# Far products of the first eight chain steps: from VectorE to GpSimd, and one order of VectorE's operations for all steps

## The chip, the cores and the metric

The kernel runs on one core of one Trainium2 chip. The core has five engines with a queue of instructions each: TensorE (PE in the profile), VectorE (DVE), ScalarE (ACT), GpSimd (POOL) and SyncE (SP, which only starts transfers here). They meet at semaphores that the program sets and waits for. The metric is the device time of one execution in microseconds. The kernel before took 275.19 us, the median of three runs (274.38 to 275.27).

## The reference, cut to what matters

The program computes two layers over 2048 tokens of width 128. Almost all of it is left alone by the change. What matters is the first layer's attention, a memory that is updated token by token:

```python
def step(M, kv):
    k_t, v_t = kv
    v_pred = jnp.einsum('bf,bfd->bd', k_t, M)
    surprise = jnp.linalg.norm(v_t - v_pred, axis=-1, keepdims=True)
    delta = k_t[:, :, None] * v_t[:, None, :]
    M = M + eta_c[None, :, None] * surprise[:, :, None] * delta
    return (_ln2(M), None)
```

`_ln2` subtracts the mean of the whole 64 x 128 matrix and divides by its deviation. Since each update is a number (the surprise) times a known outer product, the kernel never holds M in this part. It follows the surprises. They depend on inner products of keys and of values, which are known beforehand, and on the surprises of earlier tokens.

## The kernel before, in words

**Blocks side by side.** The tokens are cut into windows of L = 32 steps, which start 16 tokens apart (HALF = 16); each of the 128 partitions follows one window from a fresh start. That the windows agree where they overlap is tested afterwards (`agree`), with a general token-by-token path behind it that isn't taken. So the recurrence of 2048 tokens is a chain of 32 steps, `for j in range(L)`, with one window in each partition.

**A step of the chain.** In step j VectorE does one `tensor_tensor_scan` (L1627), which takes 18 rows of the state ST from position j to j+1 with the surprise `SG[:, j]` as factor. ScalarE waits for the scan (`scan_ready`), takes a root (L1124), and waits for VectorE's `alpha` (L1636), one number per partition; a further root gives the next surprise (L1129, `g_ready`). VectorE's remaining operations in a step spread the new surprise to later positions: `near_pairs` (L1595) adds surprise x OJN to the table Y for pairs in the same half of the window, `squares` (L1603) multiplies two rows of Y, `rows` (L1608) adds surprise x Cr to rows of ST, `mean_terms` (L1613) forms three small products. Nearly all of them read two tensors in SBUF.

**Far pairs.** Pairs with one position in the first half and one in the second are summed on TensorE. For j < FAR = 13, VectorE forms the *far product* of step j (L1690): VC[:, j] spread over 16 columns, times aT[:, j, 16:32] spread over 31 - j rows, times the surprise, (31 - j) x 16 elements, into one of three buffers FPf. TensorE adds it to PSUM bank 4 with an identity matmul (L639, `far_done`). VectorE reads the sum in step 13 (L1670, L1672), where it waits for all 13 (`far_done`, FAR).

**What sets the order.** The orders are written out by hand, one queue per engine.

- VectorE, steps j < 13: near_pairs(j), scan(j), squares(j), alpha(j), rows(0, 4), far product, mean_terms. The near pairs of a step stand ahead of its scan. From step 14 on it is another order: scan, alpha, near_pairs, rows(1, 4), squares, mean_terms, rows(0, 1), with the scan after it waiting for that last one. From step 22 on near_pairs stands ahead of alpha again, and parts of the queries (L1576) are added.
- TensorE, in step j < 13: wait for the far product, add it, then a hidden product of the expert (j < 4), then the shift matmuls `behind(k)` of `BEHIND_AT`, which carry tables of one half to the other (L607 to L617), then for j = 9 a piece of the expert's output.
- ScalarE, in step j: the roots, then `hidden` (j < 8) and copies of the shifted tables from PSUM (`BEHIND_COPY`, from j = 8).
- GpSimd does nothing between its memsets and small preparations, which end at 24.3 us, and the second layer's weights at 97.1 us.

Before the chain VectorE forms the products OJN (L1547) and OJF (L1562). Behind it stand the check of the windows, the memory's output (TensorE, L669) and the second layer from about 91 us on, where TensorE is the busiest engine.

Of the kernel before, what the change touches and what calls it, by code (L numbers as in the profile page):

```python
# [6 lines left out]
ALU = mybir.AluOpType  # L7
# [10 lines left out]
HALF = 16  # L18
S = T // HALF
L = 2 * HALF  # L20
W = S
# [26 lines left out]
FAR_BANK = 4  # L48
N_FP = 3
SB_AT = 3  # L50
LATENT = 22
# [31 lines left out]
def program(nc, a, out):  # L83
    with ExitStack() as ctx:
# [35 lines left out]
        def take(n):  # L120
            at[0] += n
            return arena[:, at[0] - n:at[0]]
# [68 lines left out]

        FPf = [take((L - 1) * HALF) for _ in range(N_FP)]
        OJF = [take((L - 1 - j) * HALF).rearrange("p (l t) -> p l t", t=HALF) for j in range(FAR, HALF)]
        b2rest = take(2 * D)[0:1].rearrange("p (i d) -> p i d", i=2)
# [53 lines left out]
        def weights_with(t):  # L248
# [35 lines left out]
        scan_ready, h_ready, alpha_ready, g_ready = (sem(n) for n in ("scan_ready", "h_ready", "alpha_ready", "g_ready"))  # L284
        fp_ready, far_done, behind_done, behind_act = (sem(n) for n in ("fp_ready", "far_done", "behind_done", "behind_act"))
        gcol_done, rh_ready, rhb_done, uw_ready, mw_done, mw_act = (
# [10 lines left out]
        tab_in, small_in, h_in = sem("tab_in"), sem("small_in"), [sem(f"h_in{i}") for i in range(2)]  # L297
        var2_ready, sd2_ready, shift_ready, xn2_act, xn2_dve, xt2_done, xt2_act = (
            sem(n) for n in ("var2_ready", "sd2_ready", "shift_ready", "xn2_act", "xn2_dve", "xt2_done", "xt2_act"))
        wvo_done, wvo_act, turn_done, skip_done, skip_act, rope_dve, turned_dve, turned_pool = (  # L300
# [67 lines left out]

        BEHIND_AT = {6: (0,), 7: (1,), 8: (2,), 10: (3,)}
        BEHIND_COPY = {8: (0,), 9: (1,), 10: (2,), 12: (3,), 13: (4,), 14: (5,)}  # L370
# [88 lines left out]
        def _(pe):  # L459
# [175 lines left out]
            for j in range(FAR):  # L635
                if j in (0, 4):
                    pe.wait_ge(eh_act, max(j, 1))
                pe.wait_ge(fp_ready, j + 1)
                mm(PS[:, FAR_BANK, j * HALF:(L - 1) * HALF], ident, FPf[j % N_FP][:, 0:(L - 1 - j) * HALF], start=(j == 0), stop=(j == FAR - 1)).then_inc(far_done, 1)  # L639
                if j < 4:  # L640
                    expert_hidden(1, j)
                for k in BEHIND_AT.get(j, ()):
                    behind(k)
                if j in EO_EARLY:
                    pe.wait_ge(eh_act, 5)
                    expert_output(0, *EO_EARLY[j])
# [303 lines left out]
        def _(act):  # L950
# [218 lines left out]
            def deviations(c):  # L1169
                piece = slice(4 * c, 4 * c + 4)  # L1170
                act.wait_ge(var2_ready, c + 1)
                f(lnt[:, 1, piece], mv[:, piece, 1], ACT.Sqrt, bias=eps2).then_inc(sd2_ready, 1)

# [150 lines left out]
        def _(pool):  # L1324
# [30 lines left out]
            nc.gpsimd.tensor_copy(b2parts[64:65, :], b2rest[:, 1, :]).then_inc(b2_ready, 1)  # L1355
            pool.wait_ge(b2_ready, 2)

            def low_part(low, value, high, rest, cols):
# [59 lines left out]
        def _(dve):  # L1418
# [160 lines left out]
            for j in range(L):  # L1579
# [36 lines left out]
                if j == HALF:  # L1616
                    dve.wait_ge(behind_act, 9)
                if j < FAR:
                    need(added)
                    dve.wait_ge(g_ready, j + 1)  # L1620
                    added = near_pairs()
                    need(formed)
                else:
                    need(max(formed, added))
                    dve.wait_ge(g_ready, j + 1)
                c = PAD + j + 1 - 2 * R_P
# [3 lines left out]

                if j < FAR and end - j - 2 > 0:
                    formed = squares()
                def alpha():
# [4 lines left out]
                if j < FAR:  # L1638
                    alpha()
                elif j == FAR:  # L1640
                    added = near_pairs()
                    alpha()
                    linear = rows(1, 4)
                elif j < LATENT:
                    if j == HALF - 1:
                        dve.wait_ge(behind_act, 6)
                    alpha()
                    if j < HALF:
                        later = Y[:, j:L - 1, HALF:L]
                        added = did(v.scalar_tensor_tensor(out=later, in0=OJF[j - FAR], scalar=sg, in1=later, op0=ALU.mult, op1=ALU.add))  # L1650
                    else:
                        added = near_pairs()
                    linear = rows(1, 4)
                    formed = squares()
                    mean_terms(linear)
                else:
                    if nb > 0:
                        added = near_pairs()
                    alpha()
                    linear = rows(1, 4)  # L1660
                    if n > 0:
                        formed = squares()
                    mean_terms(linear)

                if j == FAR:
# [6 lines left out]
                    gy = did(v.tensor_tensor(GY, GA, far_sums[:, 0:FAR, :], ALU.mult))  # L1672
                if j > FAR:
                    need(formed)
                    formed = rows(0, 1)
                    if j >= LATENT:
                        query_sums(j - LATENT)
                    continue
                if j == FAR:
                    formed = squares()  # L1680
                    need(gy)
                    formed = did(v.tensor_reduce(ST[:, R_Q, PAD + HALF - 1:PAD + L - 1], GY.rearrange("p l t -> p t l"), AX.X, ALU.add))
# [97 lines left out]
            def variances(c):  # L1780
                need(o.n)
                for n in range(4 * c, 4 * c + 4):
                    i = v.bn_aggr(mv[:, n, :], st[:, n, :])
                    (i.then_inc(var2_ready, 1) if n == 4 * c + 3 else did(i))

            def shifts(c):
                piece = slice(4 * c, 4 * c + 4)
                dve.wait_ge(sd2_ready, c + 1)
                need(did(v.reciprocal(lnt[:, 1, piece], lnt[:, 1, piece])))
                v.scalar_tensor_tensor(out=lnt[:, 6, piece], in0=mv[:, piece, 0], scalar=-1.0, in1=lnt[:, 1, piece], op0=ALU.mult, op1=ALU.mult).then_inc(shift_ready, 1)  # L1790
# [192 lines left out]
```

## Time and profile before

| | us |
|---|---|
| median of three runs | 275.19 |
| span of the profiled execution | 273.0 |
| TensorE busy in it | 258.6 (95%) |
| VectorE busy | 215.7 (79%) |
| ScalarE busy | 192.7 (71%) |
| GpSimd busy | 100.9 (37%) |

The page has no time of the profiled execution other than its span; the rest of a run's time lies outside the first and last instruction. Busy shares are means over stages with different limits. The chain that ended last goes through TensorE for 58% of the span, VectorE 30%, ScalarE 3%, GpSimd 1%; the part of it from 44.7 to 86.6 us is the chain of 32 steps. The granted TensorE clock is 0.993 of full speed on the mean. In a timeline the first number is the start of an instruction and the second how long it took. Instructions of one engine can overlap by some hundredths, so what one costs the next is read from start to start.

### The profile page before, as it was taken

Reading aid. Unit: us, or ns where it says so; the run is one execution under the profiler, and the core shown is the slowest. Engines: PE = TensorE matmul, PEld = TensorE weight load, DVE = VectorE, ACT = ScalarE, POOL = GpSimd, SP = SyncE. Lnnn points to the kernel's source line nnn. Section 1 sums busy time; section 2 is a strip of 40 time slices with the busy share of each in tenths; the row PEclk is TensorE's granted clock in tenths of the full one; section 3 lists DMA queues with packets and bytes.
Section 4 is the critical chain, followed back from the end, with each engine's and each line's share of the span. In section 5 each row is a group of like instructions: output and inputs, shape, how many; then the busy total and the mean of one; then the engine's idle time right before and its main releaser. Section 6 shows DMA issues by size and latency. Waiting matters only on the chain.

```text
span 273.0 us, 5442 instructions
## 1 busy us (share of the span) xinstructions
PE 258.6 (95%) x1792; PEld 169.9 (62%) x1796; DVE 215.7 (79%) x733; ACT 192.7 (71%) x469; POOL 100.9 (37%) x130
## 2 busy tenths in 40 slices
PE   7899999999977889999999999999999999999993
PEld 2379945466663644967877776778786444444482
DVE  6977579999999589899899988777950798666684
ACT  1497479886656479788776789998861898777730
POOL 9314000000000067898875589599775000000000
PEclk9999999999999799999999999999999999999999
DMA  7700000000000190400000000000000000000005
GB/s 199 214 15 2 2 0 4 0 1 0 2 2 0 25 413 29 154 2 4 0 2 0 2 0 1 4 0 0 2 0 2 0 1 0 4 0 0 0 18 141
DMA packets 8303, 8.51 MB, mean 31 GB/s; under 512 B 1745, under 2 KB 7378, under 8 KB 7762
## 3 DMA queue, kind: packets, MB, share of 16 engines
q1 hardware_dynamic: 7442, 7.65, 8.7%
q10 hardware_dynamic: 832, 0.49, 0.6%
q8 instruction: 16, 0.26, 0.4%
q14 instruction: 13, 0.11, 0.1%
HBM read 7.09 MB, written 1.05 MB: 30 GB/s over the span
## 4 chain that ended last, share of the span: by engine, by line
PE 58%; DVE 30%; issue 4%; ACT 3%; DMA 2%; POOL 1%; SPq 0%; DVEq 0%; ACTq 0%; POOLq 0%
PE PS L867 10%; PE PS L866 10%; PE PS L839 7%; PE PS L816 7%; PE PS L829 4%; DVE arena L1608 3%; PE PS L501 3%; PE PS L520 3%; DVE arena L1840 2%; DVE arena L1839 2%; DVE arena L1595 2%; DVE mxb L1854 2%; DVE arena L1627 2%; DVE arena L1636 2%; DMA x<-L_attn_x 2%
## 5 line engine op out<-in xcount | busy, mean ns | idle before, releaser
L866 PE MATMUL PS<-arena 128*128 128x512 f16 x128 | 48.5, 379 | 0.0
L867 PE MATMUL PS<-arena 128*128 128x512 f16 x128 | 48.5, 379 | 0.0
L1912 DVE TENSOR_TENSOR arena<-arena 128x512 f32<-128x512 f32 x32 | 22.1, 692 | 13.0 <-ACT arena L1304 13.0
L816 PE MATMUL PS<-arena 128*128 128x512 f32 (+3 forms) x80 | 31.9, 530 | 0.3 <-ACT arena L1273 0.3
L1303 ACT ACTIVATE arena<-PS,arena 128x512 f32<-128x512 f32 x32 | 22.9, 716 | 9.1 <-PE PS L867 9.1
L1368 POOL CAST arena<-arena 128x512 f16<-128x512 f32 x2 | 1.3, 644 | 72.8 <-ACT x L1166 72.8
L1360 POOL TENSOR_TENSOR arena<-arena 128x256 f32<-128x256 f32 x32 | 21.6, 674 | 15.8 <-DVE arena L1846 13.0
L1273 ACT ACTIVATE arena<-PS,lnt 128x512 f32<-128x512 f32 (+3 forms) x40 | 24.8, 628 | 3.2 <-DVE lnt L1861 3.1
L1361 POOL TENSOR_TENSOR arena<-arena,small 128x256 f16<-128x256 f32 (+1 forms) x36 | 23.8, 661 | 2.8
L1304 ACT ACTIVATE arena<-PS,arena 128x512 f16<-128x512 f32 x32 | 22.8, 714 | 0.0
L1854 DVE TENSOR_REDUCE mxb<-PS 128x1 f32<-128x512 f32 (+3 forms) x40 | 22.1, 600 | 0.0
L866 PEld LDWEIGHTS PS<-arena 128*128 128x128 f16 x128 | 12.5, 98 | 14.7
L867 PEld LDWEIGHTS PS<-arena 128*128 128x128 f16 x128 | 12.5, 98 | 14.7
L816 PEld LDWEIGHTS PS<-arena 128*128 128x128 f32 x80 | 14.0, 191 | 12.0 <-issue 9.8
L829 PE MATMUL PS<-con,arena 128*128 128x128 f32 x136 | 19.5, 273 | 0.0
L839 PE MATMUL PS<-arena,xn 128*128 128x128 f32 x144 | 19.3, 278 | 0.0
L839 PEld LDWEIGHTS PS<-arena,xn 128*128 128x128 f32 x144 | 17.7, 191 | 1.1 <-ACT xn L1257 0.2
L839 PE MATMUL PS<-arena 128*128 128x128 f32 x128 | 17.3, 278 | 0.6 <-ACT arena L1257 0.6
L829 PEld LDWEIGHTS PS<-con,arena 128*128 128x128 f32 x136 | 15.1, 141 | 2.7 <-issue 1.9
L1883 DVE SCALAR_TENSOR_TENSOR x<-PS,lnt,x 128x128 f32<-128x128 f32 x16 | 5.6, 351 | 14.0 <-PE PS L839 13.6
L839 PEld LDWEIGHTS PS<-arena 128*128 128x128 f32 x128 | 15.6, 191 | 1.3 <-ACT arena L1257 1.0
L1840 DVE SCALAR_TENSOR_TENSOR arena<-PS,arena 128x256 f32<-128x256 f32 x32 | 15.5, 484 | 1.1
(282 smaller groups left out, 641.8 us busy)
## 6 DMA issues: line engine op xcount, KB each, us to landing
arena<-h_T SPq DMA_DIRECT2D x2, 1024.0 KB, 5.8
x<-L_attn_x SPq DMA_DIRECT2D x4, 256.0 KB, 4.5
arena<-cos SPq DMA_DIRECT2D x1, 1024.0 KB, 4.8
arena<-sin SPq DMA_DIRECT2D x1, 1024.0 KB, 7.1
arena<-w_T SPq DMA_DIRECT2D x3, 256.0 KB, 3.1
out<-arena SPq DMA_DIRECT2D x2, 256.0 KB, 2.3
con<-shape_constants ACTq DMA_DIRECT2D x1, 192.0 KB, 3.3
out<-arena SPq DMA_DIRECT2D x1, 192.0 KB, 2.1
```

Source lines behind the costliest of these rows:

```text
L816: i = mm(PS[:, k, 0:cnt * P], qT1[:, t * P:(t + 1) * P], kT1[:, c * P:(c + cnt) * P], start=True, stop=not last)
L829: i = tr(PS[:, 4 + gi % 2, (b - c) * P:(b - c + 1) * P], Pr[t % 2][:, b * P:(b + 1) * P], ident)
L839: i = mm(PS[:, 7, (t % 4) * D:(t % 4 + 1) * D], PT[t % 2][:, b * P:(b + 1) * P], V1[:, b, :], start=(b == 0), stop=(b == t))
L866: mm(bank(b), wH[:, k, m * P:(m + 1) * P], sH[:, k, cols], start=(k == 0), stop=False)
L867: i = mm(bank(b), wL[:, k, m * P:(m + 1) * P], sL[:, k, cols], start=False, stop=(k == HT4 - 1))
L1273: f(Pr[t % 2][:, c * P:(c + cnt) * P], PS[:, SCORE_BANK[gi], 0:cnt * P], ACT.Exp, scale=1.0 / D, bias=nbs[:, t:t + 1], accum_out=rsums[:, ...
L1303: f(FP[u % 4], bank(u % 8), ACT.Gelu, scale=s_[:, u % HT4:u % HT4 + 1])
L1304: f(high, bank(u % 8), ACT.Gelu, scale=s_[:, u % HT4:u % HT4 + 1]).then_inc(read, 1)
L1360: o.need(o.did(tt(rest, value, high, ALU.subtract)))
L1361: return tt(low, rest, low_scale.broadcast_to([P, cols]), ALU.mult)
L1854: i = did(v.tensor_reduce(mxb[:, gi:gi + 1], PS[:, SCORE_BANK[gi], 0:cnt * P], AX.X, ALU.max))
L1912: v.tensor_tensor(RP[m], FP[m], high, ALU.subtract).then_inc(rest_ready, 1)
```

## The change

It does four things:

1. For steps j < FAR_POOL = 8 GpSimd forms the far product. It waits for the surprise, multiplies the 16 entries of aT by it (`far_scaled`), waits for that, and multiplies by VC with both operands spread, into the same three buffers. From step 8 on VectorE still forms it, now into buffers of their own in VXf, without a wait for `far_done`.
2. VectorE's operations of the steps j < 13 take the order of the later ones: scan, alpha, near_pairs, rows(1, 4), (far product for j >= 8), squares, mean_terms, rows(0, 1).
3. TensorE waits for the far product behind the other work of its step, and the `behind` pieces stand two steps earlier. The one semaphore `fp_ready` is now two, `fp_pool` and `fp_dve`.
4. In the second layer's normalisation `var2_ready` and `sd2_ready` are counted on in `var_ready` and `sd_ready`.

```diff
+FAR_POOL = 8
+        FP_AT = [sum((L - 1 - i) * HALF for i in range(FAR_POOL, j)) for j in range(FAR_POOL, FAR)]
+        def far_buffer(j):
+            n = (L - 1 - j) * HALF
+            return FPf[j % N_FP][:, 0:n] if j < FAR_POOL else VXf[:, FP_AT[j - FAR_POOL]:FP_AT[j - FAR_POOL] + n]
...
-        BEHIND_AT = {6: (0,), 7: (1,), 8: (2,), 10: (3,)}
+        BEHIND_AT = {4: (0,), 5: (1,), 6: (2,), 8: (3,)}
...
-                pe.wait_ge(fp_ready, j + 1)
-                mm(PS[:, FAR_BANK, j * HALF:(L - 1) * HALF], ident, FPf[j % N_FP][:, 0:(L - 1 - j) * HALF], start=(j == 0), stop=(j == FAR - 1)).then_inc(far_done, 1)
                 if j < 4:
                     expert_hidden(1, j)
                 for k in BEHIND_AT.get(j, ()):
                     behind(k)
+                (pe.wait_ge(fp_pool, j + 1) if j < FAR_POOL else pe.wait_ge(fp_dve, j - FAR_POOL + 1))
+                mm(PS[:, FAR_BANK, j * HALF:(L - 1) * HALF], ident, far_buffer(j), start=(j == 0), stop=(j == FAR - 1)).then_inc(far_done, 1)
...
+            for j in range(FAR_POOL):
+                pool.wait_ge(lanes_act, 4)
+                pool.wait_ge(g_ready, j + 1)
+                o.need(o.did(nc.gpsimd.tensor_scalar(far_scaled[:, j, :], CC[:, 0, j + 1, HALF:L], SG[:, j, 1:2], None, ALU.mult)))
+                pool.wait_ge(tables_ready, 1)
+                if j >= N_FP:
+                    pool.wait_ge(far_done, j - N_FP + 1)
+                sh = [W, L - 1 - j, HALF]
+                tt(far_buffer(j).rearrange("p (l t) -> p l t", t=HALF), VC[:, j, j:L - 1].unsqueeze(2).broadcast_to(sh),
+                   far_scaled[:, j, :].unsqueeze(1).broadcast_to(sh), ALU.mult).then_inc(fp_pool, 1)
...
-                if j < FAR:
-                    need(added)
-                    dve.wait_ge(g_ready, j + 1)
-                    added = near_pairs()
-                    need(formed)
-                else:
-                    need(max(formed, added))
-                    dve.wait_ge(g_ready, j + 1)
+                need(max(formed, added))
+                dve.wait_ge(g_ready, j + 1)
...
-                if j < FAR and end - j - 2 > 0:
-                    formed = squares()
...
                 if j < FAR:
                     alpha()
+                    added = near_pairs()
+                    linear = rows(1, 4)
+                    if j >= FAR_POOL:
+                        vc_, a_ = far_factors(j)
+                        v.scalar_tensor_tensor(out=far_buffer(j).rearrange("p (l t) -> p l t", t=HALF), in0=vc_, scalar=sg, in1=a_,
+                                               op0=ALU.mult, op1=ALU.mult).then_inc(fp_dve, 1)
+                    formed = squares()
+                    mean_terms(linear)
...
-                if j > FAR:
+                if j != FAR:
                     need(formed)
                     formed = rows(0, 1)
...
-                formed = rows(0, 4 if j < FAR else 1)
-                if j < FAR:
-
-                    if j >= N_FP:
-                        dve.wait_ge(far_done, j - N_FP + 1)
-                    vc_, a_ = far_factors(j)
-                    v.scalar_tensor_tensor(out=FPf[j % N_FP][:, 0:(L - 1 - j) * HALF].rearrange("p (l t) -> p l t", t=HALF), in0=vc_, scalar=sg, in1=a_,
-                                           op0=ALU.mult, op1=ALU.mult).then_inc(fp_ready, 1)
-                    formed = mean_terms(formed)
+                formed = rows(0, 1)
```

## Rows read from the trace of the kernel before

**Rows 1.** Busy time by stretch: us, then busy us (x instructions) by engine, clock, DMA.

```profile
core 0: us, PE busy (x) PEld busy (x) DVE busy (x) ACT busy (x) POOL busy (x), PEclk, DMA share, GB/s
44.70:57.09 12.39, 12.39 (x32) 5.67 (x31) 12.39 (x57) 10.71 (x35) 0.00 (x0) 1.00 0.01 2
```

**Rows 2.** Waits from 44 to 64 us: total, times, longest.

```profile
PEld PS L639 <- DVE arena L1690: 1.6, 5, 0.4
```

**Rows 3.** Timeline of VectorE, steps 0, 8 and 13 (start us, us, line, shape).

```profile
44.70 0.44 DVE L1595 SCALAR_TENSOR_TENSOR arena<-arena 128x210 f32<-128x210 f32 x1 [0.22 <-DVE arena L1567]
45.06 0.19 DVE L1627 TENSOR_TENSOR_SCAN arena<-arena 128x18 f32<-128x18 f32 x1
...
45.67 0.73 DVE L1690 SCALAR_TENSOR_TENSOR arena<-arena 128x496 f32<-128x496 f32 x1
46.32 0.16 DVE L1613 TENSOR_TENSOR arena<-arena 128x3 f32<-128x3 f32 x1
...
57.09 0.19 DVE L1627 TENSOR_TENSOR_SCAN arena<-arena 128x18 f32<-128x18 f32 x1
...
57.67 0.59 DVE L1690 SCALAR_TENSOR_TENSOR arena<-arena 128x368 f32<-128x368 f32 x1
58.19 0.15 DVE L1613 TENSOR_TENSOR arena<-arena 128x3 f32<-128x3 f32 x1
...
63.44 0.20 DVE L1627 TENSOR_TENSOR_SCAN arena<-arena 128x18 f32<-128x18 f32 x1
...
64.36 0.51 DVE L1670 SCALAR_TENSOR_TENSOR arena<-arena,PS 128x288 f32<-128x288 f32 x1
```

**Rows 4.** Timeline of VectorE, step 16, and the scan of step 21.

```profile
69.00 0.20 DVE L1627 TENSOR_TENSOR_SCAN arena<-arena 128x18 f32<-128x18 f32 x1
69.23 0.22 DVE L1636 SCALAR_TENSOR_TENSOR arena<-arena 128x1 f32<-128x1 f32 x1
69.37 0.43 DVE L1595 SCALAR_TENSOR_TENSOR arena<-arena 128x210 f32<-128x210 f32 x1
69.72 0.26 DVE L1608 SCALAR_TENSOR_TENSOR arena<-arena 128x45 f32<-128x45 f32 x1
69.89 0.18 DVE L1603 TENSOR_TENSOR arena<-arena 128x28 f32<-128x28 f32 x1
...
70.38 0.20 DVE L1627 TENSOR_TENSOR_SCAN arena<-arena 128x18 f32<-128x18 f32 x1
...
75.55 0.20 DVE L1627 TENSOR_TENSOR_SCAN arena<-arena 128x18 f32<-128x18 f32 x1
```

**Rows 5.** GpSimd's groups by line and shape: busy us, mean ns | idle before.

```profile
L1360 POOL TENSOR_TENSOR arena<-arena 128x256 f32<-128x256 f32 x32 | 21.6, 674 | 15.8 <-DVE arena L1846 13.0 <-ACT arena L1285 0.6 <-POOL arena L1361 0.5
...
L1360 POOL TENSOR_TENSOR arena<-xT,arena 128x512 f32<-128x512 f32 x4 | 4.6, 1160 | 0.6
```

**Rows 6.** Timeline of ScalarE, the surprises of steps 0 and 1.

```profile
41.85 0.21 ACT L1066 ACTIVATE arena<-arena 128x6 f32<-128x6 f32 x1
...
45.64 0.39 ACT L1129 ACTIVATE arena<-arena 128x6 f32<-128x6 f32 x1
```

**Rows 7.** The casts of L1846: ns shortest/median/longest.

```profile
L1846 DVE CAST arena<-arena x20: 293/346/1179, 134.4 to 201.9; 128x256 f16<-128x256 f32 x20
```

**Rows 8.** Timeline of VectorE and GpSimd where both are at work.

```profile
97.68 1.49 POOL L1369 TENSOR_SCALAR arena<-arena 128x512 f16<-128x512 f32 x1
...
98.67 0.16 DVE L1790 SCALAR_TENSOR_TENSOR lnt<-mv,lnt 128x4 f32<-128x4 f32 x1
...
103.48 0.69 DVE L1824 TENSOR_TENSOR arena<-arena 64x512 f32<-64x512 f32 x1
...
103.60 1.70 POOL L1375 TENSOR_TENSOR arena<-arena 64x512 f32<-64x512 f32 x1 [2.33 <-DVE arena L1822]
...
144.71 0.61 POOL L1361 TENSOR_TENSOR arena<-arena,small 128x256 f16<-128x256 f32 x1
...
144.83 0.64 DVE L1846 CAST arena<-arena 128x256 f16<-128x256 f32 x1
```

**Rows 9.** Timeline of TensorE, three far products in a row.

```profile
54.25 2.29 PE L639 MATMUL PS<-arena,con 128*128 128x432 f32 x6
```

More of the change, by code:

```diff
@@ L192, in program @@
         FPf = [take((L - 1) * HALF) for _ in range(N_FP)]
+        FP_AT = [sum((L - 1 - i) * HALF for i in range(FAR_POOL, j)) for j in range(FAR_POOL, FAR)]
+        def far_buffer(j):
+            n = (L - 1 - j) * HALF
+            return FPf[j % N_FP][:, 0:n] if j < FAR_POOL else VXf[:, FP_AT[j - FAR_POOL]:FP_AT[j - FAR_POOL] + n]
+        far_scaled = VXf[:, FP_AT[-1] + L * HALF:FP_AT[-1] + L * HALF + FAR_POOL * HALF].rearrange("p (j t) -> p j t", t=HALF)
         OJF = [take((L - 1 - j) * HALF).rearrange("p (l t) -> p l t", t=HALF) for j in range(FAR, HALF)]
@@ L284, in program @@
         scan_ready, h_ready, alpha_ready, g_ready = (sem(n) for n in ("scan_ready", "h_ready", "alpha_ready", "g_ready"))
-        fp_ready, far_done, behind_done, behind_act = (sem(n) for n in ("fp_ready", "far_done", "behind_done", "behind_act"))
+        fp_pool, fp_dve, far_done, behind_done, behind_act = (sem(n) for n in ("fp_pool", "fp_dve", "far_done", "behind_done", "behind_act"))
         gcol_done, rh_ready, rhb_done, uw_ready, mw_done, mw_act = (
@@ L297, in program @@
         tab_in, small_in, h_in = sem("tab_in"), sem("small_in"), [sem(f"h_in{i}") for i in range(2)]
-        var2_ready, sd2_ready, shift_ready, xn2_act, xn2_dve, xt2_done, xt2_act = (
-            sem(n) for n in ("var2_ready", "sd2_ready", "shift_ready", "xn2_act", "xn2_dve", "xt2_done", "xt2_act"))
+        shift_ready, xn2_act, xn2_dve, xt2_done, xt2_act = (
+            sem(n) for n in ("shift_ready", "xn2_act", "xn2_dve", "xt2_done", "xt2_act"))
         wvo_done, wvo_act, turn_done, skip_done, skip_act, rope_dve, turned_dve, turned_pool = (
@@ L1170, in deviations @@
                 piece = slice(4 * c, 4 * c + 4)
-                act.wait_ge(var2_ready, c + 1)
-                f(lnt[:, 1, piece], mv[:, piece, 1], ACT.Sqrt, bias=eps2).then_inc(sd2_ready, 1)
+                act.wait_ge(var_ready, 2 + c + 1)
+                f(lnt[:, 1, piece], mv[:, piece, 1], ACT.Sqrt, bias=eps2).then_inc(sd_ready, 1)
             def normed(c):
@@ L1678, in _ @@
                     continue
[L1679 to L1682, printed above, removed]
+                formed = squares()
+                need(gy)
+                formed = did(v.tensor_reduce(ST[:, R_Q, PAD + HALF - 1:PAD + L - 1], GY.rearrange("p l t -> p t l"), AX.X, ALU.add))
                 need(formed)
-                formed = rows(0, 4 if j < FAR else 1)
-                if j < FAR:
-                    if j >= N_FP:
-                        dve.wait_ge(far_done, j - N_FP + 1)
-                    vc_, a_ = far_factors(j)
-                    v.scalar_tensor_tensor(out=FPf[j % N_FP][:, 0:(L - 1 - j) * HALF].rearrange("p (l t) -> p l t", t=HALF), in0=vc_, scalar=sg, in1=a_,
-                                           op0=ALU.mult, op1=ALU.mult).then_inc(fp_ready, 1)
-                    formed = mean_terms(formed)
+                formed = rows(0, 1)
             query_sums(9, 10)
@@ L1783, in variances @@
                     i = v.bn_aggr(mv[:, n, :], st[:, n, :])
-                    (i.then_inc(var2_ready, 1) if n == 4 * c + 3 else did(i))
+                    (i.then_inc(var_ready, 1) if n == 4 * c + 3 else did(i))
             def shifts(c):
                 piece = slice(4 * c, 4 * c + 4)
-                dve.wait_ge(sd2_ready, c + 1)
+                dve.wait_ge(sd_ready, 2 + c + 1)
                 need(did(v.reciprocal(lnt[:, 1, piece], lnt[:, 1, piece])))
```

## The prediction

> **What bounds the kernel now.** The page's chain (the table above) names TensorE first and VectorE second over the whole span, so I looked next at which of them sets the pace in the stretch that is changed. The table by stretch says: in the 12.39 us of the first eight steps VectorE is busy 12.39 us, in 57 instructions, and GpSimd not at all [rows 1]. TensorE reads as full there too, but a busy TensorE is not one at its peak. The table of waits has it standing 1.6 us in five waits for VectorE's products [rows 2], so it follows VectorE. Each step of the chain is thus the sum of VectorE's start-to-start distances, and I read everything else from the timeline. Step 0 runs from the near pairs at 44.70 through the scan at 45.06 to the far product at 45.67, whose successor starts at 46.32. The scan of step 8 is at 57.09, that of step 13 at 63.44 [rows 3]. What follows the chain starts when the chain ends and is not touched, so a microsecond on the chain is one in the time. The profile's span is 273.0 us; the runs' median is 275.19, 2.2 us more, which I take to lie around any span of this kernel.
>
> **The change, part by part.**
>
> 1. Eight products leave VectorE, and the order becomes that of the later steps. What such a step costs can be read, since steps 16 to 20 already run it with the same near-pair sizes (210 to 110): scan 69.00, alpha 69.23, near pairs 69.37, rows 69.72, squares 69.89, next scan 70.38, so 1.38 us; five of them end at 75.55, 6.55 us in all [rows 4]. Steps 0 to 4 have 93 elements in the linear rows where step 16 has 45, and 31 in the last row where it has 15. The products give the price of an element: 496 of them hold the engine 0.65 us, 368 of them 0.52 (57.67 to 58.19) [rows 3], 1 ns each. That adds 0.05 and 0.02 a step: 6.55 + 5 x 0.07 = 6.90. Steps 5 to 7 have 90, 72 and 56 near-pair elements: 1.29, 1.27, 1.25, together 3.8. So from 44.70, where step 0 now begins with its scan, to the scan of step 8 it is 10.7 us, and 12.39 before: **-1.7 us**. It is not 8 x 0.6 because two distances open. In the old order squares stood between scan and alpha; now alpha waits for the scan (0.23). The product stood behind the rows; now the last row is a further instruction and the scan waits for it, squares to scan 0.49 with three instructions in it.
>
> 2. Steps 8 to 12 keep the product on VectorE and take the new order, which costs without return. Step 8: 0.23 + 0.14 (alpha), near pairs of 42 elements 0.35 - 0.17 = 0.18, linear rows of 69 elements 0.17 + 0.02 = 0.19, product 0.52, then 0.49 to the scan: 1.75. The product shrinks by 16 elements a step and the near pairs too: 1.75, 1.71, 1.68, 1.64, 1.61 = 8.4 us, and 63.44 - 57.09 = 6.35 before [rows 3, 4]: **+2.05 us**. The two together are +0.35.
>
> 3. GpSimd's work. For each of the eight steps it waits for g, scales 16 elements, then multiplies 496 down to 384 elements (mean 440). Its multiply takes 1.16 us for 512 elements and 0.67 for 256 [rows 5], 1.9 ns an element with 0.19 to begin: 0.22 us for the small one, 1.13 for the first large one and 1.01 on average for the seven after it, 8.2 us for the eight. If nothing on VectorE notices, this is free: 1.25 to 1.4 us a step on an engine that idles there.
>
> 4. Does VectorE notice? This is where the sum is decided. GpSimd gets g at the same time as VectorE. The ScalarE operation that makes it starts at 45.64 and takes 0.39, which is 0.97 after the scan [rows 6], while VectorE still has rows to do, so the large multiply falls on VectorE's busy part each time. The trace has three kinds of overlap. First, the casts at L1846: 0.29 us alone, 1.18 at the longest; the one at 144.83 under a GpSimd multiply from 144.71 to 145.32 takes 0.64 and ends 0.15 after it [rows 7, 8]. Nothing is shared there: the cast stands until the other is finished. Second, the addition at L1824 reads two SBUF tensors, as all of VectorE's chain operations do: it starts at 103.48, GpSimd's at 103.60, and GpSimd's takes 1.70 us instead of 1.16 [rows 5, 8]. The excess 0.54 is about what VectorE had left (to 104.17, 0.57). So an operation with two SBUF inputs and a GpSimd multiply exclude each other too, shown with VectorE first. Third, against it: at 98.67 a VectorE operation of 4 elements with two SBUF inputs took 0.16 us inside a GpSimd tensor-scalar from 97.68 to 99.17 [rows 8]. The added multiply resembles the first two cases in kind (two inputs, hundreds of elements) and the added scaling the third. So I take: each large multiply holds VectorE for its own duration, the small one for nothing. Bounds per step: below, 0; the waits that VectorE has in any case (0.11 before alpha, about 0.15 before the scan) can lie under it, 0.26 off; above, 1.28 for a form at GpSimd's slowest pace (L1369, 1.49 us for 512) plus the 0.22 of the scaling. Value taken: 1.13 + 7 x 1.01 = **+8.2 us**. The first already falls ahead of the chain, since surprise 0 is made at 41.85 [rows 6], into the products that VectorE forms before 44.70.
>
> The Trainium skill states a rule on this, in "SBUF — State Buffer", section "Who interferes with whom": a VectorE instruction with two SBUF inputs contends with a GpSimd instruction that reads SBUF, and the one that starts second waits for the whole of the other; with one SBUF input it doesn't contend. By that rule the price is the one just taken; without it, it is 0 and the time that of rival A. The trace agrees with the rule in the rows of L1846 and L1824 and differs from it in the 4-element row.
>
> 5. TensorE. The same 13 products, and the shift matmuls two steps earlier, ahead of the wait. It had waits to spare [rows 2]; three products of 432 to 400 columns take it 2.29 us, 0.76 each [rows 9]. The last must be in PSUM for the read at 64.36 [rows 3], about 0.9 after scan 13. Product 12 now lies ahead of squares, mean and row, so it comes earlier against the scan. Cost 0; with the cover gone, below. With three buffers GpSimd's step j waits for TensorE's product j-3, which at 2.4 us a step is long done. The semaphores merged for the second normalisation keep every wait at the same event: 0.
>
> Sum: -1.7 + 2.05 + 8.2 = +8.55 on the span, 281.5; the time 275.19 + 8.55 = **283.7 us**. The likeliest case's own range is 281.6 (8 x 0.26 less) to 287.6 (8 x (1.28 - 1.02) + 8 x 0.22 more).
>
> **The rivals.**
> *A: only VectorE-first excludes; GpSimd's reads never stop VectorE.* Its place is the same port, its price 0, and it decides if the first near-pair operation under a GpSimd multiply keeps its 0.44 us. For: the 4-element row. Against: the casts. Then only the reordering is left, +0.35: 275.5, not slower by a measurable amount.
> *B: A, and GpSimd starves.* VectorE's two-input operations push each multiply back, by most of one of its steps (1.2 us) at worst; GpSimd takes 1.25 + 1.2 = 2.45 us a step, eight from 42 to 61.6. TensorE's products 7 to 12 come behind it, 6 x 0.76 [rows 9] and two other pieces of its queue that size, to 67.7. They are wanted 0.9 after scan 13, at 44.7 + 10.7 + 8.4 + 0.9 = 64.7: 3 us late, 278.5. For: 1.70 instead of 1.16. Against: the chain's operations are short and waits lie between them.
> *C: the reordering pays.* If the waits that open in steps 8 to 12 are covered by the product, these steps cost only the additional row (0.1 each, +0.5): -1.2, and without blocking 274.0. Against: a wait for the instruction directly ahead cannot be covered by one further up.
> *D: GpSimd's broadcast form is far slower than the plain multiply* (2 us each): +16, 291.
> *The products don't leave VectorE as said*: excluded by the diff, the loop for j under 8 issues none.
>
> **How the numbers follow.** Blocked, 0.60; A 0.22; B 0.08; C 0.05; D 0.05. A measurement of this kernel tells about 0.3% (0.8 us) from no change. Faster: C and a sliver of A, 0.06. Same: A, 0.20. Slower: 0.74. The range has to reach A's time on one side and the dear end of the likeliest on the other: 275.2 to 287.6, leaving out C, D and part of A.
>
> **What would show it.** Steps 0 to 7: scan to scan 2.3 to 2.5 us, with one VectorE operation a step drawn out to 0.5 us or more that ends with a GpSimd multiply (right), or 1.25 to 1.45 us with every operation at its old duration (A). Scan 8 near 63.6 against 57.1. Steps 8 to 12 at 1.6 to 1.75 in every case; if they stay at 1.2 to 1.33, part 2 is wrong. The PSUM read at L1670 with an idle time before it means B. GpSimd multiplies over 1.2 us with nothing beside them mean D. The forecast is wrong as a whole if VectorE's busy time rises by less than 3 us in the chain.

## The result: 4.4 us slower, half of what was forecast

| | before | after |
|---|---|---|
| median of the runs, us | 274.88 (4 runs, 274.38 to 275.27) | 279.28 (4 runs, 278.74 to 279.6) |
| span of the profiled execution, us | 273.0 | 277.5 |
| VectorE busy in it, us | 215.7 | 220.1 |
| GpSimd busy in it, us | 100.9 | 111.3 |
| scan of step 0, 8, 13, 31 starts at | 45.06, 57.09, 63.44, 86.53 | 45.67, 60.71, 69.03, 91.92 |

The ratio after to before is 1.016, 95% interval 1.0139 to 1.0182. Forecast were 283.7 us and +8.5; it came to +4.4, inside the outer range given (275.2 to 287.6) but below the likeliest case's own (281.6 to 287.6). The direction was right and the size was about twice too large.

The chain that ended last, from the page of after, now has VectorE for 33% of the span and GpSimd for 6%:

```profile
PE 51%; DVE 33%; POOL 6%; issue 3%; ACT 3%; DMA 2%; DVEq 0%; SPq 0%; POOLq 0%; ACTq 0%
```

The busy time by stretch (columns as in [rows 1]) for the stretch of [rows 1], then for steps 0 to 7 and steps 8 to 12 of after:

```profile
44.70:57.09 12.39, 12.39 (x33) 5.93 (x32) 11.77 (x47) 8.47 (x27) 6.79 (x11) 1.00 0.00 0
45.67:60.71 15.04, 14.07 (x42) 6.97 (x40) 14.48 (x56) 9.97 (x33) 8.91 (x15) 1.00 0.00 1
60.71:69.03 8.32, 5.38 (x14) 2.25 (x14) 7.97 (x41) 5.42 (x23) 0.00 (x0) 1.00 0.00 0
```

VectorE has little idle time, as before, but in the stretch of [rows 1] it gets through 47 instructions instead of 57. Its eight steps still have 56 instructions, one product less and one row more in each; they now take 15.04 us from scan to scan, against 12.03 (45.06 to 57.09). The large operations are gone, and what is left takes longer. The timeline says which part. VectorE and GpSimd in after, ahead of the chain and in steps 0 to 2 (L1643 scan, L1650 alpha, L1617 near pairs; L1371 GpSimd's scaling, L1377 its multiply), then the scans of steps 8 and 13:

```profile
42.36 0.70 POOL L1371 TENSOR_SCALAR arena<-arena 128x16 f32<-128x16 f32 x1 [18.34 <-ACT arena L1076]
43.15 1.04 POOL L1377 TENSOR_TENSOR arena<-arena 128x496 f32<-128x496 f32 x1
43.18 1.05 DVE L1582 TENSOR_TENSOR arena<-arena 128x16 f32<-128x16 f32 x1
...
45.67 0.20 DVE L1643 TENSOR_TENSOR_SCAN arena<-arena 128x18 f32<-128x18 f32 x1 [0.20 <-DVE arena L1589]
45.91 0.22 DVE L1650 SCALAR_TENSOR_TENSOR arena<-arena 128x1 f32<-128x1 f32 x1
46.04 0.43 DVE L1617 SCALAR_TENSOR_TENSOR arena<-arena 128x210 f32<-128x210 f32 x1
...
46.77 0.33 POOL L1371 TENSOR_SCALAR arena<-arena 128x16 f32<-128x16 f32 x1 [2.58 <-ACT arena L1139]
...
47.12 0.20 DVE L1643 TENSOR_TENSOR_SCAN arena<-arena 128x18 f32<-128x18 f32 x1
47.19 1.00 POOL L1377 TENSOR_TENSOR arena<-arena 128x480 f32<-128x480 f32 x1
47.35 0.85 DVE L1650 SCALAR_TENSOR_TENSOR arena<-arena 128x1 f32<-128x1 f32 x1
48.13 0.40 DVE L1617 SCALAR_TENSOR_TENSOR arena<-arena 128x182 f32<-128x182 f32 x1
...
49.16 0.20 DVE L1643 TENSOR_TENSOR_SCAN arena<-arena 128x18 f32<-128x18 f32 x1
...
60.71 0.19 DVE L1643 TENSOR_TENSOR_SCAN arena<-arena 128x18 f32<-128x18 f32 x1
...
69.03 0.20 DVE L1643 TENSOR_TENSOR_SCAN arena<-arena 128x18 f32<-128x18 f32 x1
```

Read it in two steps. First look for an operation whose duration doesn't fit its size. The addition of 16 elements at L1582 takes 1.05 us, and alpha, one element per partition, 0.85 us instead of 0.22. In all of steps 1 to 7 alpha takes 0.79 to 0.87 us, and every other VectorE operation keeps its old duration. Then look at what else ends there: the multiply that began at 43.15 ends at 44.19 and L1582 at 44.23; the one from 47.19 ends at 48.19 and alpha at 48.20. A held operation is counted as busy, so no table of waits shows this.

Step 0 has no multiply beside it and takes 45.67 to 47.12, 1.45 us, which is the forecast figure to the hundredth. Steps 8 to 12 take 8.32 us against 8.4 forecast.

### The profile page after: what moved, and what is told of

Same layout as the page of the kernel before. It is cut to its first block, busy times and chain, and to the rows that moved or that the text cites. A ratio compares the mean times of both kernels' runs of the same rounds, so it can differ in the third digit from the quotient of the medians.

```text
span 277.5 us, 5478 instructions
## 1 busy us (share of the span) xinstructions
PE 259.9 (94%) x1792; PEld 169.1 (61%) x1796; DVE 220.1 (79%) x738; ACT 192.8 (69%) x469; POOL 111.3 (40%) x146
## 3 DMA queue, kind: packets, MB, share of 16 engines
HBM read 7.09 MB, written 1.05 MB: 29 GB/s over the span
## 4 chain that ended last, share of the span: by engine, by line
PE 51%; DVE 33%; POOL 6%; issue 3%; ACT 3%; DMA 2%; DVEq 0%; SPq 0%; POOLq 0%; ACTq 0%
PE PS L876 10%; PE PS L877 10%; PE PS L849 7%; PE PS L826 6%; DVE arena L1630 4%; DVE arena L1650 4%; PE PS L839 4%; PE PS L511 3%; POOL arena L1382 3%; POOL arena L1383 3%; PE PS L530 3%; DVE arena L1643 2%; DVE arena L1617 2%; DVE mxb L1867 2%; DMA x<-L_attn_x 2%
## 5 line engine op out<-in xcount | busy, mean ns | idle before, releaser
L476 PE MATMUL PS<-warm 128*128 128x512 bf16 x38 | 13.1, 477 | 4.1 <-DVE arena L1643 1.7
```

## The experiments

Each kernel takes apart one claim. The starts of the scans are the yardstick, since nothing behind the chain moves them. They come from one profiled execution of each kernel, and they repeat well: where two kernels do the same up to a scan they agree within 0.05 us (scan 8 of after at 60.71, of after with the old order behind it at 60.70). Each ratio is against runs of before on the same chip.

| kernel | scan 0 | scan 8 | scan 13 | time, us (ratio to before) |
|---|---|---|---|---|
| before | 45.06 | 57.09 | 63.44 | 274.88 |
| after | 45.67 | 60.71 | 69.03 | 279.28 (1.0139 to 1.0182) |
| new order alone | 44.81 | 60.18 | 68.51 | 280.05 (1.0168 to 1.0213) |
| GpSimd's products alone | 45.97 | 59.61 | 65.97 | 277.11 (1.0054 to 1.0116) |
| after, old order in steps 8 to 12 | 45.62 | 60.70 | 67.06 | 277.51 (1.0084 to 1.013) |
| TensorE's order and semaphores alone | 45.08 | 57.11 | 63.47 | 274.60 (0.9975 to 1.003) |
| after, ScalarE scales | 46.00 | 61.42 | 69.73 | 279.85 (1.0132 to 1.0247) |
| GpSimd's products alone, seven | 45.20 | 59.65 | 66.00 | 276.49 (1.0046 to 1.0095) |

**The new order alone.** Against after, GpSimd's loop goes, and VectorE forms all 13 products, into the three buffers FPf (the lines that name the buffer and TensorE's semaphore are left out here):

```diff
-            for j in range(FAR_POOL):
...
-                    if j >= FAR_POOL:
+                    if True:
+                        if j >= N_FP:
+                            dve.wait_ge(far_done, j - N_FP + 1)
```

> The order of the changed kernel in all steps, all 13 far products on VectorE, none on GpSimd. Port theory (a GpSimd multiply holds up VectorE's next operation with two SBUF inputs, and the order costs by itself): no operation drawn out; steps 0 to 7 of 1.45 to 1.25 us plus a product of 0.65 to 0.53, 15.4 us to the scan of step 8 (at 60.1), steps 8 to 12 as in the changed kernel, 8.3 us, scan 13 at 68.4; time 4 to 5 us over before, about that of the changed kernel. Rival (the loss is all GpSimd's, the order is free or pays): scan 13 near 63.4, time within 1 us of before.

Measured: nothing is drawn out, 15.37 us from scan 0 to 8, 8.33 us from 8 to 13, scan 13 at 68.51. Step 1, from the product on (L1648 product, L1613 squares, L1623 mean terms, L1618 last row, L1631 scan):

```profile
47.81 0.71 DVE L1648 SCALAR_TENSOR_TENSOR arena<-arena 128x480 f32<-128x480 f32 x1
48.44 0.18 DVE L1613 TENSOR_TENSOR arena<-arena 128x26 f32<-128x26 f32 x1
48.53 0.16 DVE L1623 TENSOR_TENSOR arena<-arena 128x3 f32<-128x3 f32 x1
48.65 0.25 DVE L1618 SCALAR_TENSOR_TENSOR arena<-arena 128x30 f32<-128x30 f32 x1
48.93 0.20 DVE L1631 TENSOR_TENSOR_SCAN arena<-arena 128x18 f32<-128x18 f32 x1
```

VectorE does the same operations as in the kernel before and one more a step (the last row by itself), and they cost 5.07 us more at scan 13, by their order alone. With GpSimd's products on top, scan 13 moves only from 68.51 to 69.03: they take 8 products off VectorE and give nothing back for it. In time the two kernels can't be told apart (the intervals of their ratios overlap).

The two prices don't simply add. The order costs 5.07 us with the products on VectorE, and 3.06 with the first eight on GpSimd (69.03 against 65.97, the next kernel). GpSimd's products cost 2.53 us in the old order (65.97 against 63.44) and 0.52 in the new. So the order is at least as large a part of the loss as GpSimd's products, whichever is counted first.

**GpSimd's products alone.** VectorE keeps the order of before, without the eight products (some lines are joined here):

```diff
-                need(max(formed, added))
-                dve.wait_ge(g_ready, j + 1)
+                if j < FAR:
+                    need(added); dve.wait_ge(g_ready, j + 1)
+                    added = near_pairs(); need(formed)
+                else:
+                    need(max(formed, added)); dve.wait_ge(g_ready, j + 1)
...
+                if j < FAR:
+                    if end - j - 2 > 0:
+                        formed = squares()
+                    alpha()
+                    need(formed)
+                    formed = rows(0, 4)
...
+                    formed = mean_terms(formed)
+                    continue
```

> GpSimd forms the first eight products as in the changed kernel, but VectorE keeps the order of before in all 13 steps. Port theory: the multiply starts 0.55 us after g, right behind the scan, and holds squares and with it alpha; g of the next step comes about 1.45 + 0.72 us after this one, so steps of about 2.1 us, and 1.2 to 1.33 us in steps 8 to 12: scan 8 near 61.5, scan 13 near 68, time 4 to 5 us over before. Rival (the order alone costs and GpSimd's work is beside it): steps of 1.33 us or less, bounded by the way from scan to g, scan 8 near 55.5, time 1.5 us under before.

Measured: 277.11 us, less than expected; steps 0 to 7 take 13.64 us instead of 12.03. VectorE in steps 0, 1 and 6, and GpSimd beside it in step 1:

```profile
46.33 0.34 DVE L1630 SCALAR_TENSOR_TENSOR arena<-arena 128x124 f32<-128x124 f32 x1
46.71 0.17 DVE L1635 TENSOR_TENSOR arena<-arena 128x3 f32<-128x3 f32 x1
46.99 0.41 DVE L1617 SCALAR_TENSOR_TENSOR arena<-arena 128x182 f32<-128x182 f32 x1
47.06 0.56 POOL L1371 TENSOR_SCALAR arena<-arena 128x16 f32<-128x16 f32 x1 [2.94 <-ACT arena L1139]
47.31 0.19 DVE L1649 TENSOR_TENSOR_SCAN arena<-arena 128x18 f32<-128x18 f32 x1
...
47.70 1.17 POOL L1377 TENSOR_TENSOR arena<-arena 128x480 f32<-128x480 f32 x1
48.04 0.85 DVE L1635 TENSOR_TENSOR arena<-arena 128x3 f32<-128x3 f32 x1
...
57.28 0.32 DVE L1630 SCALAR_TENSOR_TENSOR arena<-arena 128x100 f32<-128x100 f32 x1
57.63 0.17 DVE L1635 TENSOR_TENSOR arena<-arena 128x3 f32<-128x3 f32 x1
57.94 0.28 DVE L1617 SCALAR_TENSOR_TENSOR arena<-arena 128x56 f32<-128x56 f32 x1
```

Two readings. The hold fell on another operation than I expected: GpSimd's small scaling took 0.56 us here, so the multiply came after alpha, and in step 1 the three-element products at L1635 were held (0.85 us), in later steps these, the rows or the scan. And a product taken out is worth less than its 0.65 us: step 0, with no multiply beside it, takes 1.34 us against 1.65. What stood in the product's shadow comes out: rows to mean terms 0.38, mean terms to near pairs 0.28, where the next instruction in [rows 3] follows the product without a gap. The product shrinks from step to step and this stretch doesn't: from the rows to the next near pairs it is still 0.66 us in step 6 (57.28 to 57.94), where before took 0.85. So a product taken out is worth 0.32 us in step 0 and 0.19 in step 6; over the eight steps that makes about 2.0 us (an estimate, 0.66 against before's distance in each step), all that this offload can bring in the old order. Seven holds then cost 13.64 - 12.03 + 2.0 = 3.6 us, 0.5 each.

**After with the old order in steps 8 to 12.** The same branch, for `FAR_POOL <= j < FAR` only.

> The changed kernel with steps 8 to 12 in the order of before. Port theory: nothing changes up to scan 8 at 60.7, then 6.35 instead of 8.3 us to scan 13, at 67.1: 2.0 us under the changed kernel, 277.3. Rival (steps 8 to 12 are slow because TensorE or buffers are late, not by their order): no gain, 279.3.

Measured: 277.51 us; steps 8 to 12 take 6.36 us, scan 13 comes 1.97 us earlier. Part 2's term stands by itself.

**TensorE's order and the semaphores alone.** The kernel before with these lines, and with the product's matmul behind `expert_hidden` and `behind(k)`:

```diff
-        BEHIND_AT = {6: (0,), 7: (1,), 8: (2,), 10: (3,)}
+        BEHIND_AT = {4: (0,), 5: (1,), 6: (2,), 8: (3,)}
...
-                act.wait_ge(var2_ready, c + 1)
+                act.wait_ge(var_ready, 2 + c + 1)
...
```

> The kernel before with only the moves beside VectorE: TensorE's wait behind the other work of its step, the shift matmuls two steps earlier, the two semaphores merged. Both theories: scans at the times of before within 0.05 us, time within 0.8 us of before. If it is over 1 us slower, part of the loss lies in TensorE's queue.

Measured: no difference, and the scans within 0.03 us. Part 5's zero holds.

**What holds VectorE: five probes.** The kernel before, with GpSimd given in steps 0 to 7, behind the surprise, the scaling of 16 elements and one operation into memory that nothing reads. VectorE keeps all its work and its order. Each probe ran once, so only its scans are read, not its time. (The code is cut and shortened. Left out are the waits that guard the memory and the merged semaphores of part 4 of the change, which all five have.)

```diff
+            for j in range(8):
+                pool.wait_ge(lanes_act, 4); pool.wait_ge(g_ready, j + 1); pool.wait_ge(tables_ready, 1)
+                o.need(o.did(nc.gpsimd.tensor_scalar(aside[:, 1100:1116], CC[:, 0, j + 1, HALF:L], SG[:, j, 1:2], None, ALU.mult)))
+                # one of:
+                tt(aside[:, 0:(L-1-j)*HALF] ..., VC[:, j, j:L-1] ..., aside[:, 1100:1116] ..., ALU.mult)   # multiply
+                tt(aside[:, 0:15*HALF] ..., VC[:, j, j:j+15] ..., aside[:, 1100:1116] ..., ALU.mult)       # half the size
+                nc.gpsimd.memset(aside[:, 0:1090], 0.0)                                                    # memset
+                nc.gpsimd.tensor_copy(aside[:, 0:850], xrT[:, 0:850])                                      # copy
+                nc.gpsimd.tensor_scalar(aside[:, 0:256].bitcast(F16), xrT[:, 0:512], 1.0 / LOW, None, ALU.mult)
```

The multiply:

> The kernel before, with GpSimd's scaling and multiply of the changed kernel added for steps 0 to 7, results unused (written aside); all products stay on VectorE. Port theory: one VectorE operation per step (scan or squares) drawn out to about 0.85 us, ending within 0.05 us of GpSimd's multiply; scan 8 about 0.97 + 7 x 0.65 = 5.5 us later than before, at 62.6. Rival (GpSimd's work is beside VectorE's): scan 8 at 57.1, every VectorE operation at its old duration.

The memset:

> As p1, but in place of the multiply a memset of 1090 elements, about 1.0 us as well, which reads nothing. Port theory in the form 'the read side is what is fought for': no VectorE operation drawn out, scan 8 within 0.2 us of before (57.1 to 57.3). Rival form 'any GpSimd operation holds VectorE': scan 8 near 62.6.

The copy:

> As p1, but in place of the multiply a copy of 850 elements, about 1.0 us, with one input in SBUF. If any GpSimd read holds the port: scan 8 near 62.5, as in p1. If it takes a GpSimd operation with two inputs: scan 8 near 57.1. I expect the first, with less certainty than p1 (0.65).

The tensor-scalar:

> As p1, but in place of the multiply the form under which the 4-element operation of before was not held: a GpSimd tensor-scalar of 512 elements f32 to f16, 1.49 us there. If it holds the port for its whole time: about 1.2 us a step, scan 8 near 66. If this form doesn't (as that row suggests): scan 8 near 57.1, and the row was about the form. If it holds VectorE here, the row was about the small size or the moment.

The multiply of 240 elements:

> The kernel before with the second normalisation's semaphores merged, and beside it on GpSimd in steps 0 to 7 the scaling of 16 entries and a broadcast multiply of 240 elements (0.65 us by the line 0.19 + 1.9 ns an element) into memory that nothing reads. The probe with 496 to 384 elements cost 5.9 us at scan 8. If the hold goes by the multiply's duration: one VectorE operation a step drawn out by about 0.4 us less than there, scan 8 at 57.1 + 8 x 0.35 = 59.9 (59.3 to 60.5). If each clash had a fixed price: scan 8 near 62.9 as there. If only multiplies of more than some 256 elements exclude VectorE: 57.3.

Scan 8 came at 62.95 with the multiply, 57.31 with the memset, 62.70 with the copy, 59.98 with the tensor-scalar and 60.19 with the half multiply, against 57.09. For the tensor-scalar that is neither of the times I had expected. One step of each, GpSimd's operation and the VectorE operation beside it. Multiply:

```profile
47.60 1.08 POOL L1367 TENSOR_TENSOR arena<-arena 128x480 f32<-128x480 f32 x1
47.75 0.98 DVE L1616 TENSOR_TENSOR arena<-arena 128x26 f32<-128x26 f32 x1
```

Memset, with squares and alpha under it at their usual durations:

```profile
46.82 1.01 POOL L1366 MEMSET arena<- 128x1090 f32 x1
46.99 0.19 DVE L1614 TENSOR_TENSOR arena<-arena 128x26 f32<-128x26 f32 x1
47.10 0.22 DVE L1647 SCALAR_TENSOR_TENSOR arena<-arena 128x1 f32<-128x1 f32 x1
```

Copy, which has one input:

```profile
47.47 0.89 POOL L1366 COPY arena<-arena 128x850 f32<-128x850 f32 x1
47.52 0.89 DVE L1638 TENSOR_TENSOR_SCAN arena<-arena 128x18 f32<-128x18 f32 x1
```

Tensor-scalar, float32 to float16:

```profile
47.21 1.57 POOL L1366 TENSOR_SCALAR arena<-arena 128x512 f16<-128x512 f32 x1
47.36 0.58 DVE L1614 TENSOR_TENSOR arena<-arena 128x26 f32<-128x26 f32 x1
47.87 0.21 DVE L1647 SCALAR_TENSOR_TENSOR arena<-arena 128x1 f32<-128x1 f32 x1
48.00 0.33 DVE L1619 SCALAR_TENSOR_TENSOR arena<-arena 128x120 f32<-128x120 f32 x1
```

Half the multiply:

```profile
47.12 0.68 POOL L1367 TENSOR_TENSOR arena<-arena 128x240 f32<-128x240 f32 x1
47.27 0.57 DVE L1616 TENSOR_TENSOR arena<-arena 128x26 f32<-128x26 f32 x1
```

It is GpSimd's reading of SBUF that holds VectorE. An operation of the same length that only writes (memset) costs next to nothing: 12.10 us from scan 0 to 8 against 12.03, and that includes the scalings, so they don't hold VectorE either. A copy with one input costs about as much as the multiply, 16.84 - 12.03 = 4.81 us, 0.69 each. It goes by duration: seven multiplies of 0.95 us on the mean cost 16.97 - 12.03 = 4.94 us between scans 0 and 8, 0.71 each; seven of 0.63 us cost 14.70 - 12.03 = 2.67, 0.38 each. Both are the duration less a quarter of a microsecond. So neither a fixed price a clash nor a threshold at 256 elements fits. And the tensor-scalar lasts 1.57 us but holds only in its first part: alpha starts 0.66 us after it, 0.56 in a later step (57.09 and 56.53), and alpha and the rows run under the rest at full pace. A hold costs 0.35 to 0.45 us there. That is what the 4-element row of [rows 8] showed: it came 0.99 us into such an operation. I had read it as evidence against a hold; it was evidence about that one operation's second part.

**After, with the scaling on ScalarE.**

```diff
+                    if j + 1 < FAR_POOL:
+                        act.wait_ge(g_ready, j + 2)
+                        f(far_scaled[:, j + 1, :], CC[:, 0, j + 2, HALF:L], ACT.Copy, scale=SG[:, j + 1, 1:2]).then_inc(scaled_act, 1)
...
-                o.need(o.did(nc.gpsimd.tensor_scalar(far_scaled[:, j, :], CC[:, 0, j + 1, HALF:L], SG[:, j, 1:2], None, ALU.mult)))
+                pool.wait_ge(scaled_act, j + 1)
```

> The changed kernel, but ScalarE multiplies the 16 entries by the surprise, right behind the operation that makes it, and GpSimd issues one instruction a step. Port theory: what VectorE pays is the part of GpSimd's multiply that doesn't lie under the scan and the waits; without GpSimd's own scaling (0.33 us and a gap) the multiply starts up to 0.2 us earlier against the scan or at the same time, so the hold a step is 0.4 to 0.65 us (more of it under the wait for the surprise) if the scan is not held, or 0.75 to 0.85 if the multiply comes ahead of the scan and holds it too: scan 8 between 60.2 and 61.8, time 279 to 280.5. Rival (it is GpSimd's number of instructions and their chain that delays the step): scan 8 below 59, time under 277.5.

Measured: scan 8 at 61.42, 279.85 us. Not faster with one GpSimd instruction a step less, so the rival falls. Steps 3 to 7, where the pattern is settled, take 9.07 us against 9.54 in after: ScalarE's scaling takes 0.31 us, nearly what GpSimd's did (0.33), but the multiply now starts with the scan and more of it lies under scan and wait.

```profile
52.35 0.20 DVE L1648 TENSOR_TENSOR_SCAN arena<-arena 128x18 f32<-128x18 f32 x1
52.37 0.99 POOL L1382 TENSOR_TENSOR arena<-arena 128x448 f32<-128x448 f32 x1 [1.48 <-ACT arena L1146]
52.58 0.79 DVE L1655 SCALAR_TENSOR_TENSOR arena<-arena 128x1 f32<-128x1 f32 x1
```

What it wins there it loses at the start: scan 1 comes 2.05 us after scan 0, not 1.45, and scan 2 another 2.92 after that. The scan of step 1 waits 0.65 us for ScalarE, which is at its four copies of 512 elements from 45.32 to 47.37 (in after from 43.48 to 45.53); it was already 1.4 us later than in after when it loaded its function table ahead of the first surprise, and I didn't trace why. In step 1 two operations are held, near pairs (1.21) and the last row (0.96).

**GpSimd's products alone, product 0 left on VectorE.**

```diff
-            for j in range(FAR_POOL):
+            for j in range(1, FAR_POOL):
...
-                    if j >= FAR_POOL:
+                    if j >= FAR_POOL or j == 0:
```

> The kernel with GpSimd's products and VectorE's order of before, but product 0 stays on VectorE (GpSimd forms seven, steps 1 to 7). The chain then starts as before (scan 0 at 45.1 instead of 45.97, -0.9), step 0 has its product back (+0.55 at most): scan 8 at 59.6 - 0.3 to 59.6 - 0.9 = 58.7 to 59.3, time 276.3 to 276.8, against 277.1 with eight. Rival (the hold ahead of the chain is not what delayed it): scan 0 stays at 45.9 and the time is 277.5.

Measured: scan 0 at 45.20, as expected: the first multiply did cost 0.77 us ahead of the chain. But scan 8 is at 59.65, no earlier than with eight (59.61). Step 0 has its product back (+0.32), and the multiply of step 1 now starts with the scan (46.83 and 46.86) instead of behind alpha, and holds squares for 0.98, +0.25 in that step; the later steps are 0.24 longer together. The price of a hold moves by 0.2 us with where it falls, which I had not foreseen. The time is 276.49, inside what was expected, but that is luck: the stretch behind the chain was 208.5 us here and 209.1 with eight, and the times of the two kernels can't be told apart (the intervals of their ratios overlap).

No kernel here beats the one before.

## Why the prediction was right and wrong

**What bounds it.** Right: the chain's length went straight into the span, 5.59 us at scan 13 and 4.5 in the span. It isn't one for one. The span behind scan 13 is 209.56 us in before and 208.47 in after, and in the other kernels, which don't touch it, 208.3 to 209.2. It varies by itself. Of the 1.1 us, 0.2 went between scans 13 and 31 (23.09 and 22.89), and 0.5 at the memory's output: there the same eight matmuls took 1.23 us in before (at 88.63), in a stretch at a granted clock of 0.50 (the 1.2 GHz level), and 0.71 us in after (at 94.01), at 1.00 (2.4 GHz). In before the clock fell behind 6.5 us in which TensorE was busy 4.18 (80.0 to 86.5); in after it still stood behind 6.0 us with 3.79 busy (86.0 to 92.0), and fell in the stretch behind these matmuls. Why it fell earlier in the one than in the other no run here shows. TensorE in before and in after, then the clock by stretch, first before, then after (columns as in [rows 1]):

```profile
88.63 1.23 PE L669 MATMUL PS<-arena 64*128 64x128 f32 x8 [0.19 <-ACT arena L1146]
94.01 0.71 PE L679 MATMUL PS<-arena 64*128 64x128 f32 x8 [0.19 <-ACT arena L1156]
```

```profile
88.60:89.90 1.30, 1.27 (x10) 1.02 (x10) 0.45 (x3) 0.00 (x0) 0.00 (x0) 0.50 0.00 0
93.90:94.70 0.80, 0.69 (x10) 0.57 (x10) 0.51 (x3) 0.06 (x1) 0.00 (x0) 1.00 0.00 0
94.70:97.30 2.60, 2.45 (x28) 2.25 (x28) 0.89 (x5) 0.60 (x1) 0.00 (x0) 0.64 0.03 6
```

The remaining 0.4 us lies in the 180 us behind that; I didn't trace it. My line "a microsecond on the chain is one in the time" is good to about 0.6 us on either side, no better.

**Parts 1 and 2, the order.** Right. A step without a product and without a hold is seen by itself only once: 1.45 in step 0, as forecast. The new order's worth in the whole is seen without GpSimd: 15.37 and 8.33 us. Rival C (the reordering pays) is refuted by the new order alone and by the old order put back in steps 8 to 12. The forecast nonetheless hid the weight of this part: I booked products gone and new order together as -1.7 for the eight steps. Taken apart, the order costs 15.37 - 12.03 = 3.34 us there, and the absent products give 15.37 - 10.7 = 4.7 (10.7 is the forecast's own figure, which step 0 bears out: 1.45 us with the product gone, 2.09 with it). In the old order the same products give only about 2.0.

**Part 3, GpSimd's pace.** Nearly right. The seven multiplies take 1.00 down to 0.84 us, 0.92 on the mean, where 1.01 was forecast; the broadcast form is no slower than the plain one (rival D falls). The scaling takes 0.33 to 0.38 us, and 0.70 the first time, not 0.22.

**Part 4, the hold.** This is the step that failed, by its size. The kind was right: one operation a step is drawn out and ends with GpSimd's multiply, in after and in two probes, so rival A falls. So does B: the multiplies aren't pushed back (0.92 us on the mean, eight ending at 59.91), and from scan 13 to scan 14, with the read of PSUM in between, it is 2.54 us (69.03 to 71.57), as in before (63.44 to 66.00). But the term "each large multiply holds VectorE for its own duration", +8.2 us, was too large by 3.0. Measured are 0.86 ahead of the chain (45.67 against 44.81 in the new order alone) and (15.04 - 10.7) / 7 = 0.62 in each of seven steps, 4.3 us: 5.2 in all. That 0.62 doesn't hang on the 10.7: from alpha to the near pairs it is 0.13 us in step 0 and 0.76 on the mean of steps 1 to 7, 0.63 more. The 0.39 a step between 1.01 and 0.62 is made of three pieces, on the mean of the seven steps. 0.09: the multiply is shorter than forecast. 0.10: it begins while VectorE is at the scan or waits, until alpha starts (0.16 us in step 1, 47.19 to 47.35, and 0.07 or less from step 4 on). 0.20: the held operation ends with the multiply (48.20 and 48.19) instead of beginning there, so its own 0.13 to the next instruction lies under it, and that next one, the near pairs at 48.13, starts 0.06 ahead of the multiply's end. The third I could have read from [rows 8]: the cast ended 0.15 after the multiply, and alone it takes 0.29, so it too overlapped by half its length. For the lower end of the likeliest case's range I had taken off 0.26 a multiply, the waits alone, and had nothing for the other two.

One more reading there was wrong. The cast of L1846 has a single input, so the rule as I cited it (with one SBUF input VectorE doesn't contend) speaks against its hold, though I counted it as agreeing. The Trainium skill's sentence, in "SBUF — State Buffer", section "Who interferes with whom", says this of one input outside VectorE's 2-port modes only; no run here shows in which mode the cast ran.

The scaling, booked at nothing, was right in effect: behind the memsets the same scalings cost 0.07 us over seven steps, and in after it only delays the multiply, by 0.42 us from its own start, which put it under the scan.

**Part 5.** Right: zero.

**The sum, redone with what was measured:** scan 13 at 44.81 + 0.86 + 15.04 + 8.32 = 69.03; against 63.44 it is +5.59; less 1.1 us behind the chain +4.5 in the span, +4.4 in time. Of the 4.1 us by which the forecast was too high, 3.0 are the hold and 1.1 the stretch behind the chain, which no term had.

**The signs on record.** The drawn-out operation that ends with a GpSimd multiply is there in every step from 1 to 7. The steps take 1.85 to 2.05 us, not 2.3 to 2.5, and scan 8 stands at 60.71, not near 63.6: the same error of size. VectorE's busy time in the chain (to scan 13) rose from 18.71 to 22.45 us, more than the 3 us under which the forecast would have been wrong as a whole.

## What to carry to other kernels

An engine that idles is no free place for work if its reads of SBUF hold up the busy engine. Compare the time that an operation would hold the busy engine from outside (0.38 to 0.71 us here) with what taking it off that engine brings. That is not its duration but what is left when the waits in its shadow come out: of 0.65 us it was 0.64 in the new order (step 0, 2.09 against 1.45) and 0.32 down to 0.19 in the old one. Where the hold isn't clearly smaller, leave it. And when a change removes work and reorders at once, price the two apart: here the order alone cost 5.07 us in the chain, and the joint term of -1.7 hid it.

## What the hardware showed that I had not expected

- A GpSimd copy with one input (0.89 us) holds VectorE's two-input operations just as a two-input multiply does (0.69 and 0.71 us a step); a memset of 1.01 us doesn't. No run here puts a VectorE operation with one input in their place.
- A GpSimd tensor-scalar of 512 float32 into float16 lasts 1.5 us and holds VectorE in about its first 0.6 us only. Its reported duration says little of the hold.
- Whether an operation that starts within 0.1 us of GpSimd's is held varies: the scan at 47.52 behind a copy from 47.47 was (0.89 us), the scan at 47.12 ahead of a multiply from 47.19 wasn't, and in the multiply probe a scan at 47.63 behind a multiply from 47.60 wasn't either. With GpSimd's seven products, rows that started at 54.75, ahead of a multiply from 54.78, were held (1.04 us). The exact moment at which the reading begins stays open.
- The Trainium skill's rule in "SBUF — State Buffer", section "Who interferes with whom" (a VectorE instruction with two SBUF inputs waits for the whole of a GpSimd instruction that reads SBUF) gave the right pair of operations, copy and memset included. On the length the traces agree for the multiplies, where the held operation ends with GpSimd's, though it costs less than their duration (0.38 of 0.63 us, 0.71 of 0.95), since its own work lies under the hold. They differ for the tensor-scalar, about 0.6 of 1.5 us, and the rows at 54.75 started first and were held all the same.
